# Low-rank attention of a two-layer kernel: score matmuls as 64-row pairs, four banks for key scores and three shared ones, 1024-column exponentials, softmax totals inverted as 128x8 through DMA

## The chip, the cores and the metric

The kernel runs on one core of a Trainium2 chip, as one program. The metric is the device time of one execution in microseconds; lower is better. TensorE is called PE below, VectorE DVE, ScalarE ACT, GpSimd POOL, and SyncE (which issues DMAs) SP.

## What is computed

Two layers over x of shape (8, 1024, 128): a window attention with 16 heads of 8 dimensions and a gated low-rank feed-forward part, then a low-rank attention and a feed-forward part whose input is quantised in blocks of 32. The change is in the second layer's attention. The reference has batches of (b, s) = (8, 1024) there and 8 heads:

```python
c_q = h_t @ W_DQ + b_DQ
c_kv = h_t @ W_DKV + b_DKV
q_c = (c_q @ W_UQ + b_UQ)...; k_c = (c_kv @ W_UK + b_UK)...; v_c = (c_kv @ W_UV + b_UV)...
q_r = (c_q @ W_QR + b_QR)...; k_r = (h_t @ W_KR + b_KR)   # the same for all heads
scores = jnp.einsum('bhsd,bhtd->bhst', concat(q_c, q_r), concat(k_c, k_r)) / sqrt(160)
attn = jax.nn.softmax(scores, axis=-1)
o = jnp.einsum('bhst,bhtd->bhsd', attn, v_c)
return o.reshape(b, s, 1024) @ W_O + b_O
```

The kernel folds the up-projections into the queries and into the output weights, so that a head's score is a product over 64 numbers (32 of c_kv and 32 of k_r) plus a constant for each query, and a head's result has 32 numbers before the output projection. Queries and keys stand as a high and a low part in a reduced-precision float, whose products are added.

## The kernel before

The program is written engine by engine, with semaphores between the queues; each queue runs in the order in which it is written. The gated part and the window attention take the first 580 us or so; the low-rank attention takes the rest and is the part that changes. In it the kernel goes through 64 heads u = 0..63 (8 batches of 8), each in 8 tiles of 128 keys, so that step g = 8u + t is tile t of head u. A plan (`low_rank_plan`) adds to the steps the small work of the other parts of the layer: "turn", "low", "const" and "value" prepare the next batch, "proj" is the output projection, "quant" and "product" the feed-forward part, "norm" and "quantise" their normalisations.

In step g each engine does the following:

- PE computes row scores (`pe_row_scores`, L1825) 14 steps ahead (`ROW_LEAD`), with the queries on the partitions: two matmuls of 512 columns for each tile of 128 queries. From them only the maximum over the keys is taken. It computes the key scores of step g (`pe_key_scores`, L1878 and L1882), with the keys on the partitions: for each half of the queries one matmul over 128 rows (high and low key parts against the high query part) and one over 65 rows (high key part against the low query part, and a row of ones against the shift). Every fourth step it weighs the values with four tiles of exponentials (`pe_weigh`, L1936), and at t = 3 of the next head it also sums the exponentials of a head over the keys ("total", L1929), which the plan places ahead of that weighing.
- DVE takes the maxima (`dve_row_max`, L1833, two per step), gathers them (`dve_row_top`, L1841), makes the low query part (L1754), inverts the totals (`dve_invert_totals`, L1946) and normalises (`dve_normalise`, L1953).
- ACT takes the exponentials (L1893, two per tile of 512 queries each) and copies the high query part out of PSUM (L1702).
- POOL adds seven of the head's eight tiles of exponentials in six additions (`pool_sum`, L1904 and L1907), and computes the shift (L1853, L1857).
- SP moves the shift into a row (`sync_move_shift`, L1864, 4 DMAs for each half of a head) and the normalised head into place (`sync_move_head`, L1964, 4 DMAs).

PSUM has 8 banks of 512 columns. Key scores go round banks 0 to 2, weighed values are in 3, row scores and totals go round 4 to 6, and bank 7 holds a query product or one of the small items. A matmul waits until the bank's last user has been read (`row_bank_free`, `low_bank_free`). Query products (L1641) are made 16 and 12 steps ahead, one half each.

## Time and profile before

| | |
|---|---|
| median of 3 runs | 1809.59 us (1809.46 to 1812.57) |
| profiled execution | span 1812.5 us; its own time is that of the slowest run shown, 1812.57 us |
| busy share of the span | PE 92%, PE weight loads 67%, DVE 77%, ACT 63%, POOL 65% |
| granted TensorE clock, mean | 0.967 of full speed |

A busy PE is not a PE at its peak: a 512-column matmul is shown as about 0.40 us while the next one starts 0.23 us later. So the cost of PE work is read below from the distance between two starts, and the same holds for DVE and ACT, whose instructions overlap a little as well.

### The profile page before, as it was taken

The page shows a single profiled execution, that of the slowest core. Times are in us where ns is not written, and L with a number is a line of the kernel's source. Part 1 is how long each engine was busy: PE and PEld are TensorE (multiplying, and loading weights), DVE is VectorE, ACT ScalarE, POOL GpSimd, SP SyncE. Part 2 cuts the span into 40 slices and gives each one's busy share as a digit, 9 for nine tenths or more (in the row PEclk, how much of TensorE's full clock was granted, in tenths as well). Part 3 has the DMA queues.
Part 4 walks back from the last instruction along what each step waited for, and adds up shares of the span by engine and source line. Part 5 has one row for each costly group of instructions (what it writes and reads, how often), then busy time and mean ns, then how long its engine had stood idle before and what let it go on. Part 6 is the DMA issues. An engine that isn't in the chain of part 4 may idle for free.

```text
span 1812.5 us, 39662 instructions
## 1 busy us (share of the span) xinstructions
PE 1670.4 (92%) x15057; PEld 1223.0 (67%) x15057; DVE 1393.8 (77%) x2976; ACT 1137.5 (63%) x2222; POOL 1177.3 (65%) x909
## 2 busy tenths in 40 slices
PE   4679999999877899999999999999999999999995
PEld 4557777777766567666766766766676677677674
DVE  5557777766597888878888888888887888888862
ACT  5447777777676466666666666666656666665662
POOL 4300111000066498898898988989889898898892
PEclk9889999999887899999999999999999999999997
DMA  4556666654000000000000000001001000100101
GB/s 123 136 140 156 162 156 159 164 136 116 29 1 1 1 10 8 10 8 10 7 13 16 10 8 19 11 7 22 7 10 19 8 10 7 22 7 10 19 10 30
DMA packets 198677, 81.47 MB, mean 45 GB/s; under 512 B 152553, under 2 KB 177493, under 8 KB 198357
## 3 DMA queue, kind: packets, MB, share of 16 engines
q1 hardware_dynamic: 198484, 78.93, 19.5%
q8 instruction: 119, 1.95, 0.5%
q14 instruction: 74, 0.60, 0.1%
HBM read 39.79 MB, written 29.88 MB: 38 GB/s over the span
## 4 chain that ended last, share of the span: by engine, by line
PE 54%; DVE 11%; POOL 2%; issue 1%; ACT 1%; DMA 0%; SPq 0%; POOLq 0%; ACTq 0%
PE pair L1825 12%; PE pair L1878 11%; PE pair L1882 11%; PE pair L1936 10%; DVE amax L1833 4%; PE pair L1929 4%; PE pair L1650 2%; DVE o_inv L1946 1%; PE pair L1641 1%; DVE stats L485 1%; POOL w_mix L1907 1%; PE pair L1664 1%; DVE q_low L1754 1%; DVE cq L1765 1%; DVE key_hl L1768 1%
## 5 line engine op out<-in xcount | busy, mean ns | idle before, releaser
L1893 ACT ACTIVATE prob<-pair 128x512 f32<-128x512 f32 x1024 | 604.4, 597 | 422.2 <-PE pair L1882 359.6
L1833 DVE TENSOR_REDUCE amax<-pair 128x1 f32<-128x512 f32 x1024 | 670.3, 682 | 133.9 <-PE pair L1825 131.8
L1825 PE MATMUL pair<-key_hl,q_hi 128*128 128x512 f32 x1024 | 437.8, 430 | 11.2 <-DVE amax L1833 7.1
L1878 PE MATMUL pair<-q_hi,key_hl 128*128 128x512 f32 x1024 | 405.2, 396 | 2.6 <-ACT prob L1893 2.6
L1882 PE MATMUL pair<-q_low,key_h 65*128 65x512 f32 x1024 | 406.0, 396 | 0.0
L1907 POOL TENSOR_TENSOR w_mix<-w_mix,prob 128x1024 f32<-128x1024 f32 x160 | 382.3, 2389 | 25.2 <-ACT prob L1893 8.5
L1907 POOL TENSOR_TENSOR Wm<-Wm,prob 128x1024 f32<-128x1024 f32 x155 | 369.6, 2384 | 20.8 <-ACT prob L1893 4.1
L520 POOL TENSOR_SCALAR veps<-mv 128x8 f32<-128x8 f32 x47 | 11.4, 243 | 452.6 <-DVE mv L493 451.2
L1825 PEld LDWEIGHTS pair<-key_hl,q_hi 128*128 128x128 f32 x1024 | 196.1, 192 | 115.9 <-issue 51.0
L1936 PE MATMUL pair<-prob,values 128*32 128x256 f32 x4096 | 247.2, 382 | 0.0
L1186 DVE TENSOR_REDUCE mx_neg<-pair 128x4 f32<-128x512 f32 x256 | 164.9, 687 | 94.8 <-PE pair L1090 94.1
L1878 PEld LDWEIGHTS pair<-q_hi,key_hl 128*128 128x128 f32 x1024 | 195.5, 191 | 44.3 <-ACT prob L1893 9.4
L1882 PEld LDWEIGHTS pair<-q_low,key_h 65*128 65x128 f32 x1024 | 192.5, 188 | 44.6
L1936 PEld LDWEIGHTS pair<-prob,values 128*32 128x32 f32 x4096 | 127.5, 110 | 100.9 <-issue 25.0
L1136 ACT ACTIVATE yT<-pair 128x512 f32<-128x512 f32 x256 | 138.6, 593 | 72.3 <-PE pair L1042 70.3
L1946 DVE RECIPROCAL o_inv<-pair 128x256 f32<-128x256 f32 x64 | 112.5, 1758 | 59.8 <-PE pair L1929 59.8
L542 ACT ACTIVATE y<-x,mean_neg,rstd 128x128 f32<-128x128 f32 x336 | 137.7, 485 | 19.0 <-POOL mean_neg L528 18.9
L1090 PE MATMUL pair<-keys,queries 64*128 64x128 f32 x1024 | 100.5, 317 | 0.0
L1042 PE MATMUL pair<-queries,keys 64*128 64x128 f32 x1024 | 97.0, 309 | 0.0
L1702 ACT ACTIVATE q_hi<-pair 128x512 fp32r<-128x512 f32 x128 | 75.7, 591 | 20.0 <-PE pair L1641 20.0
L1754 DVE TENSOR_TENSOR q_low<-pair,q_hi 64x512 fp32r<-64x512 f32 x128 | 86.3, 675 | 2.2 <-ACT q_hi L1702 2.2
L1090 PEld LDWEIGHTS pair<-keys,queries 64*128 64x128 f32 x1024 | 82.7, 199 | 3.7
(209 smaller groups left out, 2232.8 us busy)
## 6 DMA issues: line engine op xcount, KB each, us to landing
rows_mem<-once SPq DMA_DIRECT2D x128, 128.0 KB, 2.0
queries<-rows_mem SPq DMA_DIRECT2D x64, 256.0 KB, 4.5
keys<-rows_mem SPq DMA_DIRECT2D x16, 1024.0 KB, 7.1
rows_mem<-once SPq DMA_DIRECT2D x128, 64.0 KB, 1.9
q_low<-shift_cols SPq DMA_DIRECT2D x512, 0.5 KB, 2.0
yT<-o_norm SPq DMA_DIRECT2D x256, 32.0 KB, 1.9
x<-x_dram SPq DMA_DIRECT2D x8, 512.0 KB, 7.3
out_dram<-x SPq DMA_DIRECT2D x7, 512.0 KB, 3.4
```

Source lines behind the costliest of these rows:

```text
L542: ins = e.activation(y_of(stage, b)[:, t, :], x[:, b * NT + t, :], ACT.Identity, bias=mean_neg[:, k, t:t + 1], scale=rstd[:, k, t:t + 1])
L1090: ins = e.matmul(bank(S_BANKS[r])[:, q * P:(q + 1) * P], queries[rows, hb % QUERY_BUFS, q, m].rearrange("p s w -> p (s w)"), keys[rows, b ...
L1136: e.activation(pT[:, u % P_TURNED].rearrange("p q k -> p (q k)"), key_row_bank(*divmod(u, 2)), ACT.Exp).then_inc(*exps.up(u))
L1186: e.tensor_reduce(mx_neg[:, hb % 2, r, :, m], bank(S_BANKS[r]).rearrange("p (q k) -> p q k", q=QUADS), AX_X, ALU.max, negate=True).then_in ...
L1825: e.matmul(row_bank(("row", r, i)), q_hi[:, k, t * P:(t + 1) * P], key_hl[:, b % 2, i * HALF:(i + 1) * HALF], start=True, stop=True, skip_ ...
L1833: e.tensor_reduce(amax1[:, u % 2, t, i:i + 1], row_bank(("row", r, i)), AX_X, ALU.max).then_inc(*row_maxed.up((r, i)))
L1878: e.matmul(bank(j), key_hl[:, b % 2, ks], q_hi[:, k, sl], start=True, stop=False, skip_group_check=True)
L1882: e.matmul(bank(j), key_h1[:, b % 2, ks], q_low[:, k, sl], start=False, stop=True, skip_group_check=True).then_inc(*key_scored.up((g, half)))
L1893: e.activation(prob1[:, g % P_BUFS, half * HALF:(half + 1) * HALF], bank(K_BANKS[(2 * g + half) % 3]), ACT.Exp, scale=SCALE1).then_inc(*ke ...
L1907: e.tensor_tensor(into, into, p, ALU.add).then_inc(*summed_keys.up(g))
L1936: ins = e.matmul(bank(PVB)[q * DC:(q + 1) * DC, 0:QUARTER], values[:, b % 2, t, :], prob1[:, g % P_BUFS, q * QUARTER:(q + 1) * QUARTER], s ...
L1946: e.reciprocal(o_inv[:, u % 2, :], row_bank(("total", u, 0))[:, 0:QUARTER]).then_inc(*o_inverse.up(u))
```

## The change

It touches the low-rank stage alone.

- **Layout.** The two halves of the 1024 queries stand above each other: `q_hi` and `q_low` are 128x512, with the first 512 queries on partitions 0 to 63 and the others on 64 to 127. `key_high` and `key_low` hold the 64 key rows twice. The shift has a tile of its own, `q_shift`, in which row 0 and row 64 hold it, and is added by a matmul against ones.
- **Scores.** All score matmuls take 64 rows and come in pairs, one on partitions 0 to 63 and one on 64 to 127, into two banks. Row scores are one pair per step where they were two full matmuls (they use the high parts alone); key scores are four pairs (high by high, low key, low query, shift) where they were two full matmuls and two of 65 rows. One query product of two accumulated matmuls serves a whole head, 17 steps ahead.
- **Banks.** Key scores of step g use two banks (0 and 1, or 2 and 3), weighed values are in 4. Banks 5 to 7 are shared in turn by row scores, totals, queries and all small items. Small items now stand only at t = 3: one ahead of the total, one behind the weighing.
- **Exponentials.** One of 1024 columns per tile, which waits for both sides.
- **Additions.** POOL adds six of the eight tiles in five additions; PE sums three parts for the total where it summed two.
- **Totals.** For all heads but the last two ACT copies totals and weighed values to SBUF. SP moves the totals into 128x8 (4 DMAs), DVE inverts that, SP stores it to DRAM (1), waits for it, and loads it back spread over 4x32 partitions (4); then DVE multiplies. Line numbers of the changed kernel in what follows: L1858 row scores, L1920 key scores, L1867 maxima, L1783 `q_low`, L2010 inversion, L2028 normalisation.

The core of the diff:

```diff
-PIPELINE = 16
+PIPELINE = 17
+PVB, SHARED_BANKS = 4, (5, 6, 7)
+SUMMED = 6
...
+    def use(key):
+        places[key] = SHARED_BANKS[len(uses) % 3], uses[-3] if len(uses) >= 3 else None
+        uses.append(key)
+        return places[key]
...
-        if item is None and waiting and (g % 2 == 0 or g >= NT * U):
+        if item is None and waiting and (g >= NT * U or g % NT == 3 and waiting[0][0] != "low"):
...
+        def pe_row_scores(e, r):
+            u, t, half = row_tiles(r)
+            b, k = u // NH, u % Q_BUFS
+            e.wait_ge(*q_hi_done.at((u, 0)))
+            if r % (NT * NH) == 0:
+                e.wait_ge(*key_copied.at((b, 1)))
+            for side in range(2):
+                shared_bank_free(e, ("row", r, side))
+            for side in range(2):
+                rows = slice(side * KR, (side + 1) * KR)
+                e.matmul(shared_bank(("row", r, side)), q_hi[rows, k, t * P:(t + 1) * P],
+                         key_high[rows, b % 2, half * HALF:(half + 1) * HALF], start=True, stop=True,
+                         skip_group_check=True).then_inc(*row_scored.up((r, side)))
...
+        def pe_key_scores(e, g):
...
+            if g >= 2:
+                e.wait_ge(*key_exp.at(g - 2))
+            for part in range(4):
+                if t == 0 and part == 2:
+                    e.wait_ge(*q_lo_done.at((u, 0)))
+                if t == 0 and part == 3:
+                    e.wait_ge(*shift_ready(u))
+                for side in range(2):
+                    rows = slice(side * KR, (side + 1) * KR)
+                    weights = ones_shift[rows, :] if part == 3 else (key_low if part == 1 else key_high)[rows, b % 2, ks]
+                    moving = (q_hi, q_hi, q_low, q_shift)[part][rows, k, :]
+                    ins = e.matmul(banks[side], weights, moving, start=part == 0, stop=part == 3, skip_group_check=True)
...
+        def act_copy_total(e, u):
+            e.wait_ge(*totalled.at(u))
...
+        def sync_move_total(e, u):
+            e.wait_ge(*total_copied.at(u))
+            for q in range(4):
+                e.dma_start(total_cols[q * DC:(q + 1) * DC, u % 2, :],
+                            total_rows[q * DC:q * DC + 1, u % 2, :].rearrange("o (p t) -> o p t", t=NT)).then_inc(
+                    total_moved[u % 2], 16)
+        def dve_invert_spread(e, u):
+            e.wait_ge(total_moved[u % 2], 64 * (u // 2 + 1))
+            e.reciprocal(inverse_cols[:, u % 2, :], total_cols[:, u % 2, :]).then_inc(*spread_inverse.up(u))
+        def sync_move_inverse(e, u):
+            e.wait_ge(*spread_inverse.at(u))
+            e.dma_start(inverse_mem[u % 2].rearrange("(p t) -> p t", t=NT), inverse_cols[:, u % 2, :]).then_inc(
+                inverse_stored[u % 2], 16)
+            e.wait_ge(inverse_stored[u % 2], 16 * (u // 2 + 1))
+            for q in range(4):
+                e.dma_start(o_inv[q * DC:(q + 1) * DC, u % 2, :],
+                            inverse_mem[u % 2, q * QUARTER:(q + 1) * QUARTER].unsqueeze(0).broadcast_to([DC, QUARTER])
+                            ).then_inc(inverse_moved[u % 2], 16)
+        def dve_normalise_spread(e, u):
+            e.wait_ge(inverse_moved[u % 2], 64 * (u // 2 + 1))
+            e.wait_ge(*o_copied.at(u))
...
+                if t == 3 and 0 <= u and spread_out(u):
+                    dve_invert_spread(e, u)
+                if t == 7 and 0 <= u and spread_out(u):
+                    dve_normalise_spread(e, u)
...
             for u in range(B * NH + 2):
                 if u < B * NH:
-                    for i in range(2):
-                        sync_move_shift(e, u, i)
+                    sync_move_shift(e, u)
                 if u >= 2:
+                    if spread_out(u - 2):
+                        sync_move_total(e, u - 2)
+                        sync_move_inverse(e, u - 2)
                     sync_move_head(e, u - 2)
```

What this does to the order, at three places. First SP, in the middle of the stage; `yT<-o_norm` moves a normalised head, `q_low<-shift_cols` moves a shift. Before, two heads:

```order
L1964 DMA yT<-o_norm 32x256 x4
L1864 DMA q_low<-shift_cols 1x128x1 x8
L1964 DMA yT<-o_norm 32x256 x4
L1864 DMA q_low<-shift_cols 1x128x1 x8
L1964 DMA yT<-o_norm 32x256 x4
```

And now, two heads from the same part of the program:

```order
L2046 DMA yT<-o_norm 32x256 x4
L1898 DMA q_shift<-shift_cols 1x128x1 x8
L2004 DMA total_cols<-total_rows 32x1x8 x4
L2015 DMA inverse_mem<-inverse_cols 128x8
L2019 DMA o_inv<-inverse_mem 32x256 x4
L2046 DMA yT<-o_norm 32x256 x4
L1898 DMA q_shift<-shift_cols 1x128x1 x8
L2004 DMA total_cols<-total_rows 32x1x8 x4
```

Per head there are 21 DMAs where there were 12, and between the moves of the shift and those of the head stand the three steps of the inversion. In `sync` the shift that follows head u's normalisation is that of head u + 3, and the totals behind it are those of head u + 1.

Second DVE, one head before:

```order
L1833 TENSOR_REDUCE amax<-pair 128x1 x4
L1946 RECIPROCAL o_inv<-pair 128x256
L1953 TENSOR_TENSOR o_norm<-pair,o_inv 128x256
L1833 TENSOR_REDUCE amax<-pair 128x1 x4
L1841 TENSOR_REDUCE shift<-amax 128x4
L1754 TENSOR_TENSOR q_low<-pair,q_hi 64x512
L1833 TENSOR_REDUCE amax<-pair 128x1 x8
L1841 TENSOR_REDUCE shift<-amax 128x4
L1754 TENSOR_TENSOR q_low<-pair,q_hi 64x512
```

And now:

```order
L2028 TENSOR_TENSOR o_norm<-o_raw,o_inv 128x256
L1867 TENSOR_REDUCE amax<-pair 128x1 x8
L2010 RECIPROCAL inverse_cols<-total_cols 128x8
L1867 TENSOR_REDUCE amax<-pair 128x1 x6
L1783 TENSOR_TENSOR q_low<-pair,q_hi 128x512
L1867 TENSOR_REDUCE amax<-pair 128x1 x2
L1874 TENSOR_REDUCE shift<-amax 128x8
L2028 TENSOR_TENSOR o_norm<-o_raw,o_inv 128x256
```

The inversion stands between the fourth and the fifth pair of maxima after a normalisation, in front of the maxima of that step, and the multiplication four steps later. One `q_low` per head stands between the seventh and the eighth pair.

Third PE, at a query product. Before, with the waits (`row_half_maxima` is the end of a maximum on DVE, `query_low` that of `q_low`):

```order
L1878 MATMUL pair<-q_hi,key_hl 128x512 [waits key_exponentials]
L1882 MATMUL pair<-q_low,key_h 128x512 [waits shift_row_1_last_half]
L1641 MATMUL pair<-cq,w_query 128x512 [waits keys_ready]
L1825 MATMUL pair<-key_hl,q_hi 128x512 [waits row_half_maxima]
L1878 MATMUL pair<-q_hi,key_hl 128x512 [waits key_exponentials]
L1882 MATMUL pair<-q_low,key_h 128x512
L1825 MATMUL pair<-key_hl,q_hi 128x512 [waits row_half_maxima]
L1878 MATMUL pair<-q_hi,key_hl 128x512 [waits key_exponentials]
```

And now, from the row scores behind the product and the weighing on:

```order
L1858 MATMUL pair<-key_high,q_hi 128x512 [waits row_half_maxima]
L1858 MATMUL pair<-key_high,q_hi 128x512
L1920 MATMUL pair<-q_hi,key_high 128x512 [waits key_exponentials]
L1920 MATMUL pair<-q_hi,key_high 128x512
L1920 MATMUL pair<-q_hi,key_low 128x512 x2
L1920 MATMUL pair<-q_low,key_high 128x512 x2
L1920 MATMUL pair<-q_shift,ones_shift 128x512 x2
L1858 MATMUL pair<-key_high,q_hi 128x512 [waits row_half_maxima,query_low]
L1858 MATMUL pair<-key_high,q_hi 128x512
```

Before, a query product had bank 7 to itself and no row score waited for it; now the second pair of row scores behind it takes its bank.

## Rows read from the trace of the kernel before

**Rows 1.** Busy time by engine (PE, PEld, DVE, ACT, POOL), clock; attention stage.

```profile
700.00:1750.00 1050.00, 1032.91 (x7965) 722.80 (x7958) 876.47 (x1554) 663.06 (x1199) 939.76 (x650) 1.00 0.08 12
```

**Rows 2.** Groups of instructions by line, 700 to 1750 us.

```profile
L1833 DVE TENSOR_REDUCE amax<-pair 128x1 f32<-128x512 f32 x914 | 599.1, 682 | 118.8 <-PE pair L1825 116.9
L1893 ACT ACTIVATE prob<-pair 128x512 f32<-128x512 f32 x914 | 541.7, 597 | 377.0 <-PE pair L1882 319.1 <-POOL Wm L1904 6.1
...
L1946 DVE RECIPROCAL o_inv<-pair 128x256 f32<-128x256 f32 x57 | 100.2, 1758 | 34.0 <-PE pair L1929 34.0
L1754 DVE TENSOR_TENSOR q_low<-pair,q_hi 64x512 fp32r<-64x512 f32 x114 | 76.9, 675 | 0.0
...
L485 DVE BATCH_NORM_STATS2 stats<-x 128x6 f32<-128x128 f32 x104 | 22.0, 274 | 0.0
...
L1768 DVE SCALAR_TENSOR_TENSOR key_hl<-pair,Wt,key_hl 64x512 fp32r<-64x512 f32 x12 | 8.9, 744 | 0.4
```

**Rows 3.** The write of o_norm: all 64, then two in the timeline.

```profile
L1953 DVE TENSOR_TENSOR o_norm<-pair,o_inv x64: 405/425/427, 637.3 to 1785.5; 128x256 f32<-128x256 f32 x64
...
709.17 0.42 DVE L1953 TENSOR_TENSOR o_norm<-pair,o_inv 128x256 f32<-128x256 f32 x1
...
725.82 0.42 DVE L1953 TENSOR_TENSOR o_norm<-pair,o_inv 128x256 f32<-128x256 f32 x1
```

**Rows 4.** Timeline of PE round a total and a weighing.

```profile
1202.60 0.39 PE L1878 MATMUL pair<-q_hi,key_hl 128*128 128x512 f32 x1
1202.83 0.39 PE L1882 MATMUL pair<-q_low,key_h 65*128 65x512 f32 x1
1203.14 0.64 PE L1929 MATMUL pair<-prob,ones_col 128*32 128x256 f32 x8
...
1204.03 1.91 PE L1936 MATMUL pair<-prob,values 128*32 128x256 f32 x32
1205.87 0.50 PE L1825 MATMUL pair<-key_hl,q_hi 128*128 128x512 f32 x1
1206.21 0.39 PE L1878 MATMUL pair<-q_hi,key_hl 128*128 128x512 f32 x1
```

**Rows 5.** Timeline of PE in the window stage, 64-row matmuls.

```profile
301.87 0.39 PE L1085 MATMUL pair<-mask_bf,both_rows 64*128 64x512 bf16 x2 [0.17 <-DVE mx_neg L1186]
301.90 0.74 PE L1090 MATMUL pair<-keys,queries 64*128 64x128 f32 x8
302.49 0.39 PE L1035 MATMUL pair<-both_rows,mask_bf 64*128 64x512 bf16 x2
```

**Rows 6.** Timelines of PE and DVE: row scores and their maxima.

```profile
1196.41 0.50 PE L1825 MATMUL pair<-key_hl,q_hi 128*128 128x512 f32 x1
...
1196.94 1.39 DVE L1833 TENSOR_REDUCE amax<-pair 128x1 f32<-128x512 f32 x2 [1.02 <-PE pair L1825]
...
1201.53 2.46 DVE L1833 TENSOR_REDUCE amax<-pair 128x1 f32<-128x512 f32 x4
...
1202.26 0.50 PE L1825 MATMUL pair<-key_hl,q_hi 128*128 128x512 f32 x1 [0.46 <-DVE amax L1833]
```

**Rows 7.** Timelines of DVE and SP, then DMA issues with us to landing.

```profile
1152.77 0.42 DVE L1953 TENSOR_TENSOR o_norm<-pair,o_inv 128x256 f32<-128x256 f32 x1
...
1153.22 2.47 SPq L1964 DMA_DIRECT2D yT<-o_norm  x4
...
1158.52 2.46 SPq L1864 DMA_DIRECT2D q_low<-shift_cols  x4
...
q_low<-shift_cols SPq DMA_DIRECT2D x512, 0.5 KB, 2.0
yT<-o_norm SPq DMA_DIRECT2D x256, 32.0 KB, 1.9
```

**Rows 8.** PE after a long wait, and the clock of that stretch (columns of rows 1).

```profile
364.06 0.61 PE L1085 MATMUL pair<-mask_bf,both_rows 64*128 64x512 bf16 x2 [2.73 <-DMA keys<-rows_mem]
...
364.00:370.70 6.70, 6.64 (x68) 5.27 (x70) 1.59 (x3) 2.76 (x7) 0.48 (x3) 0.50 0.50 123
```

More of the change, by code:

```diff
@@ L265, in low_rank_plan @@
     while g < NT * U + 26 or running or waiting:
-        early, late = [], []
+        early, late, after = [], [], []
         b, r = divmod(g, NT * NH)
@@ L1636, in pe_low_part @@
                 return
-            low_bank_free(e, before)
+            if item not in places_m or before:
+                low_bank_free(e, before)
             if kind == "query":
@@ new lines, in sync_move_shift @@
+        def sync_move_shift(e, u):
+            e.wait_ge(*shift_steps.at((u, 2)))
+            queries_free(e, u)
+            if u == 0:
+                e.wait_ge(*set_low.at("shift rows"))
+            for t in range(NT):
+                side, n = divmod(t, NT // 2)
+                e.dma_start(q_shift[side * KR:side * KR + 1, u % Q_BUFS, n * P:(n + 1) * P].bitcast(F32).rearrange(
+                    "o (p t) -> o p t", t=1), shift_cols[:, t:t + 1].bitcast(F32)).then_inc(
+                    shift_moved[u % Q_BUFS], 16)
@@ L1822, in pe_row_scores @@
+        def pe_key_scores(e, g):
+            u, t = divmod(g, NT)
+            b, k = u // NH, u % Q_BUFS
+            ks = slice(t * P, (t + 1) * P)
+            banks = [bank(g % 2 * 2 + side) for side in range(2)]
             if u % NH == t == 0:
                 e.wait_ge(*keys_done.at((b, 1)))
-            row_bank_free(e, ("row", r, i))
-            e.matmul(row_bank(("row", r, i)), q_hi[:, k, t * P:(t + 1) * P], key_hl[:, b % 2, i * HALF:(i + 1) * HALF],
-                     start=True, stop=True, skip_group_check=True).then_inc(*row_scored.up((r, i)))
@@ L1896, in pool_sum @@
+        def act_exponentials(e, g):
+            if g >= P_BUFS:
+                before = g - P_BUFS
+                e.wait_ge(*pv_done.at(before // 4))
+                if before % NT < SUMMED:
+                    e.wait_ge(*summed_keys.at(max(before % NT, 1) + before // NT * NT))
+            for side in range(2):
+                e.wait_ge(*key_scored.at((g, side)))
+            e.activation(prob1[:, g % P_BUFS, :], pair[g % 2][:, :], ACT.Exp, scale=SCALE1).then_inc(*key_exp.up(g))
         def pool_sum(e, g):
@@ L1993, in pe_low_rank @@
             e.wait_ge(*x_dve.at(("c", B - 2)))
-            for g, early, late in plan_m:
+            e.wait_ge(*keys_done.at((0, 1)))
+            for g, early, late, after in plan_m:
                 if g == CONST_AT:
@@ L2013, in pe_low_rank @@
                     pe_weigh(e, g // 4 - 1)
+                for (item, j, before), part in after:
+                    pe_low_part(e, item, j, before, part)
         def act_low_rank(e):
-            for g, early, late in plan_m:
+            for g, early, late, after in plan_m:
                 if g == LAST_C["copy"]:
@@ L2056, in dve_low_rank @@
         def dve_low_rank(e):
-            for g, early, late in plan_m:
+            for g, early, late, after in plan_m:
                 if g == CONST_AT + 1:
```

313 lines of the change are left out of this document (155 added, 158 removed).

## The prediction

> **What bounds the kernel now.** I read the table by stages first. In the steady part of the low-rank stage, 1050 of the 1812 us, PE is busy for 1033 us at the full clock; DVE is busy for 876, ACT 663, POOL 940 [rows 1] (the row gives the length, then busy us and instructions of PE, PEld, DVE, ACT and POOL, then the clock). Then I looked at what one head costs. The 64 normalisations start from 637.3 to 1785.5 us, 18.2 us apart on average, and two heads without small items are 16.65 us apart [rows 3]. Does PE's own work explain these 16.65 us? A 512-column matmul follows the last one after 0.23 us, a total costs 0.89 us (1203.14 to 1204.03), and a weighing 2.03: from the start at 1202.83 to the one at 1206.21 are 3.38 us, less 0.89 and two ordinary slots [rows 4]. A head has 16 row-score, 32 key-score and 2 query matmuls: 50 x 0.233 = 11.65, two weighings 4.06, a total 0.89, together 16.6. So a plain head waits for nothing. PE sets the pace, and the 1.6 us on top are small items with a few waits.
>
> **What the change takes from PE and adds.** The window stage has 64-row pairs already. Two 512-column matmuls of 64 rows lie within 0.39 us, the time of one, and the eight of 128 columns behind them take 0.74 us in four pairs, their weights loaded while the columns of the pair before run [rows 5]. I take 0.233 us for a pair of 512 columns, as for one full matmul. Bounds: not below this, since one matmul has that pace, and twice as much if pairs should not run side by side. Per head: row scores go from 16 slots to 8 (-1.87 us), key scores stay at 32 slots, the query at 2; the third part of the total costs half of 0.89 (+0.44). PE's part falls by 1.4 us to about 15.2 per plain head. Five additions in place of six and the cheap reciprocal relieve POOL and DVE (L1946 is 1.76 us, [rows 2]), which did not set the pace. The exponential of 1024 columns costs between one and two of 0.60 us [rows 2]; I take 1.0. With two pairs of banks, key scores of step g+2 can start 2.2 us after those of g (three slots, 0.44, 1.0, 0.05), while PE needs 2 x 1.17 = 2.33 for two steps. That is hidden.
>
> **What it adds in waits: DVE and three banks.** A maximum starts 0.03 us after the row score's end, so about 0.44 after its start (0.53 for the long one behind a weighing), four maxima take 2.46 us, so 0.60 from one to the next, and PE goes on 0.06 us after the end of the maximum that it waited for [rows 6]. A step of PE is now 5 x 0.233 = 1.17 us and its two maxima take 1.20, where before a step had 1.40. DVE has no room left between two weighings, and row scores, totals, queries and items share three banks. The eighth pair of row scores takes the query's bank, so it waits for `q_low`, which is queued behind the seventh pair's maxima: 0.44 + 2 x 0.60 + 0.68 + 0.06 = 2.38 us after the seventh pair, where PE would be there after 1.17. That stalls PE, and with it the next key scores, for 1.2 us per head. By the same steps the second pair behind a normalisation comes 0.55 late (gathering and normalisation stand ahead of the maxima), and the total, the query and the last pair before it 0.25, 0.25 and 0.15. These 2.4 us turn 15.3 into 17.7, more than the 16.65 of now.
>
> **What it adds in waits: one queue for all DMAs.** This is the larger part. Four DMAs keep SP for 2.47 us, 0.62 each, and land 1.9 to 2.0 us after their issue; the first starts 0.45 us after the start of the normalisation that it waits for [rows 7]. Let N be the start of one head's normalisation. Behind it SP issues 4 moves of the head, 8 of the next shift (ready by then, since its maxima stand ahead of N), and only then the 4 of the next head's totals. The last of the 16 is issued at N + 0.45 + 15 x 0.62 = N + 9.75 and has landed at N + 11.75, so DVE inverts at N + 11.8 at the earliest. By its own work it would be there at N + 8.3 in a plain head (my count: 4.9 us to the end of the weighing, two steps, their maxima and the queue before it). DVE waits 3.5 us. What is queued behind the wait is the fifth pair of maxima, for which PE's sixth pair waits, and all of PE with it.
>
> From the inversion I to the next normalisation there is no slack either. The store and its return and the four loads take 0.15 + 2.1 + 1.9 + 2.0 = 6.2 us, but the engines need more: the fifth pair's first maximum ends at I + 0.78 and its second at 1.38, query from 1.44 to 1.9, weighing to 3.95, key scores to 4.9, seventh pair's maxima and `q_low` to 7.2, eighth pair at 7.25, its maxima from 7.7 to 9.0, gathering, next normalisation at I + 9.1. A head therefore takes 11.8 + 9.1 = 20.9 us. Small items stand in the first part and mostly fit under SP's 11.8; the projection's two items of 1.8 us just fill it.
>
> **The sum.** Normalisations 0 to 61 go through DRAM: 61 distances x (20.9 - 18.2) = 165 us. Items that stand in the DVE part or don't fit: 14 heads with a "low" item, whose bank waits for three operations of 0.74 us [rows 2], 1.5 us each beyond SP's time; 14 heads with eight statistics and their aggregation, 1.3 us each (eight x 0.19 of the 0.27 us shown [rows 2], half of it ahead of `q_low`, and 0.5): 39 us. PE now stands still for about 3.7 us in each head. Behind a wait of 2.73 us the clock fell to half, the lower level of 1.2 GHz, for 6.7 us [rows 8]. Its price is between nothing and the 3.4 us that PE works between I and the seventh pair, x 61; since the fall comes late there and SP's part has slack at its end, I take 0.4 per head, 24 us. Total: 1812.5 + 165 + 39 + 24 = 2040 us; the profiled execution is 3 us above the median, which I leave.
>
> The Trainium skill's page "TensorE: Matmul & The Clock Gate" (section "Why this matters for your kernels") advises against idle gaps mid-kernel because the clock falls behind them; by it the 24 us would be nearer the upper bound than nothing.
>
> **The rivals.**
> - *Only the banks count* (0.12): DMAs are issued faster than I think, or the inversion is in time. Then heads take 17.7, with their items 20.3 on average (the 1.6 of now, 0.3 for switches between shapes and 1.0 for the items that share banks): 1812.5 + 61 x 2.1 = 1940. For it: the DMA's own time is short. Against it: 0.62 us of SP per DMA in every row. The Trainium skill's page "DMA: Bandwidth & Descriptors", section "Issuing engines are not separate DMA queues", calls the time to initiate a DMA usually small relative to the DMA itself. By that rule SP's chain would be three landings of 2 us and this rival would hold; the trace has 0.62 against 2.0, times sixteen.
> - *The clock falls in every head on the path* (0.12): 61 x 1.7 more instead of 24: about 2120.
> - *Pairs do not overlap* (0.03): 40 slots more per head, 9.3 us, part of it under the waits: about 2400. Rows 5 speak against it.
> - *PE stays the bound* (0.05): DVE's waits are hidden and a head costs PE's 15.3 us where it cost 16.6: 64 x 1.3 gives 1730. It needs both the wait for `q_low` (1.2 us, almost the whole gain) and the wait for the totals gone. The point that decides: 11.8 + 9.1 would have to be below 18.2, so SP below 0.45 us per DMA.
> - *Gains and waits cancel* (0.01): within 0.2%, about what a measurement of this kernel can tell from no change.
>
> **How the numbers follow.** The forecast, 0.67, has its own range of 1990 to 2090: the SP part by 0.60 to 0.65 us per DMA, the clock from nothing to 1.2 us per head. With the banks-only case and the clock case on either side the range for eight in ten is 1930 to 2130. Faster 0.05, same 0.01, slower 0.94: every other case is slower.
>
> **What would show it.** Normalisations (L2028) about 21 us apart. Reciprocals (L2010) late, their idle time put down to the DMA `total_cols`, some 3 us per head. SP with almost no wait for the shift, where issues of L2046, L1898 and L2004 stand in one row of 16 over 10 us. PE idle in front of L1858, once per head for 3 to 4 us with maxima as releaser (the step of the inversion), and once for 1.2 us with `q_low` as releaser. L1858 and L1920 in pairs, 0.23 us from pair to pair. The granted clock below 1.0 in this stage if the clock's term is there. I am wrong if heads are under 18.2 us apart, if DMAs behind one another cost SP much less than 0.6 us, or if the 16 issues don't stand between a normalisation and the next inversion.

## The result, and the profile after

The changed kernel takes 2137.6 us, the median of 4 runs (2129.2 to 2146.1), beside 1809.5 us for the kernel before (1805.7 to 1812.6): 1.181 times, with a 95% interval of 1.177 to 1.185. It is slower by 328 us. The forecast was 2040 us with a range of 1930 to 2130, so the direction was right and the time lies just above the range. The profiled execution has a span of 2127.2 us.

The windows first, with the columns of [rows 1] (the last two are for later), then the groups by line over 700 to 1750 us, and the two kinds of normalisation (count: shortest, median and longest in ns, first and last start).

```profile
700.00:1750.00 1050.00, 880.68 (x8126) 559.30 (x8128) 591.91 (x1158) 487.70 (x629) 617.94 (x378) 0.94 0.09 15
...
1521.80:1525.40 3.60, 1.01 (x4) 0.52 (x4) 1.88 (x4) 1.02 (x1) 3.46 (x2) 0.98 0.04 4
1525.40:1529.00 3.60, 3.60 (x33) 1.35 (x32) 0.77 (x2) 0.60 (x1) 0.22 (x1) 0.54 0.23 41
```

```profile
L1867 DVE TENSOR_REDUCE amax<-pair 128x1 f32<-128x512 f32 x718 | 460.5, 683 | 324.1 <-PE pair L1858 318.3
L1932 ACT ACTIVATE prob<-pair 128x1024 f32<-128x1024 f32 x358 | 366.4, 1024 | 340.7 <-PE pair L1920 333.0
...
L1783 DVE TENSOR_TENSOR q_low<-pair,q_hi 128x512 fp32r<-128x512 f32 x45 | 30.5, 679 | 0.0
...
L2010 DVE RECIPROCAL inverse_cols<-total_cols 128x8 f32<-128x8 f32 x45 | 9.0, 199 | 56.1 <-DMA total_cols<-total_rows 56.0
```

```profile
L2028 DVE TENSOR_TENSOR o_norm<-o_raw,o_inv x62: 389/424/427, 664.2 to 2085.3; 128x256 f32<-128x256 f32 x62
L2035 DVE TENSOR_TENSOR o_norm<-pair,o_inv x2: 415/420/424, 2088.4 to 2098.7; 128x256 f32<-128x256 f32 x2
```

In [rows 1] every engine but PE had idle time and PE had almost none: 1033 of 1050 us. Now PE is busy for 881, and no engine is full. 718 maxima fit in the stretch where 914 did [rows 2]. A maximum costs what it did, 683 ns; the exponential of 1024 columns costs 1.02 us; the reciprocal fell from 1.76 us to 0.20. The work is cheaper and the time is longer, so it went into waiting. The 61 distances between the normalisations of L2028 are 23.3 us on average (2085.3 less 664.2); over the same heads they were 18.4 before, and 61 times the difference is 302 us of the 328.

What PE waits for in that stretch (line waited for: us in total, times, longest):

```profile
PE pair L1858 <- DVE amax L1867: 74.1, 69, 3.8
PE pair L1858 <- DVE q_low L1783: 55.6, 45, 1.8
PE pair L1858 <- DVE key_low L1798: 30.1, 11, 2.7
PE pair L1858 <- ACT total_rows L1991: 7.0, 10, 0.7
```

And the timeline of one head on SP's queue, DVE and PE, from its normalisation at 1510.31 to the next at 1534.39:

```profile
1510.76 2.44 SPq L2046 DMA_DIRECT2D yT<-o_norm  x4
1513.30 6.24 SPq L1898 DMA_DIRECT2D q_shift<-shift_cols  x8
1519.58 2.50 SPq L2004 DMA_DIRECT2D total_cols<-total_rows  x4
1523.70 0.34 SPq L2015 DMA_DIRECT2D inverse_mem<-inverse_cols  x1
1525.13 2.52 SPq L2019 DMA_DIRECT2D o_inv<-inverse_mem  x4
...
1510.31 0.42 DVE L2028 TENSOR_TENSOR o_norm<-o_raw,o_inv 128x256 f32<-128x256 f32 x1
...
1523.47 0.20 DVE L2010 RECIPROCAL inverse_cols<-total_cols 128x8 f32<-128x8 f32 x1 [2.64 <-DMA total_cols<-total_rows]
...
1534.39 0.42 DVE L2028 TENSOR_TENSOR o_norm<-o_raw,o_inv 128x256 f32<-128x256 f32 x1
...
1524.37 0.50 PE L1858 MATMUL pair<-key_high,q_hi 64*128 64x512 f32 x2 [2.58 <-DVE amax L1867]
...
1525.71 3.38 PE L1974 MATMUL pair<-prob,values 128*32 128x256 f32 x32
```

SP issues sixteen DMAs in one piece, from 1510.76 to 1522.08, and DVE stands before the inversion until the last of them has landed. PE's row scores stand behind that in turn: at 1524.37 they start after 2.58 us with the maxima as releaser. Then the clock is at its lower level: the last two windows have 0.98 ahead of 1525.4, where PE is busy for 1.01 of 3.60 us, and 0.54 behind it. The weighing there takes 3.38 us, where one at the full clock takes 1.94 (at 1514.11 in the same head). In what follows N is a normalisation, I the next inversion and N' the next normalisation; these distances are worked out from the start times of L2028 and L2010 in the traces, as means over the 61 normalisations whose next head goes through DRAM. A head's number h is u mod 8, counted at N.

### The profile page after: what moved, and what is told of

It reads as the page before. It is cut to its first block, busy times and chain, and to the rows that moved or that the text cites. A ratio compares the mean times of both kernels' runs of the same rounds, so it can differ in the third digit from the quotient of the medians.

```text
span 2127.2 us, 45092 instructions
## 1 busy us (share of the span) xinstructions
PE 1761.2 (83%) x17673; PEld 1208.2 (57%) x17673; DVE 1255.8 (59%) x2865; ACT 1089.7 (51%) x1770; POOL 1011.5 (48%) x719
## 4 chain that ended last, share of the span: by engine, by line
PE 39%; SPq 22%; DVE 16%; issue 8%; DMA 7%; ACT 5%; POOL 4%; POOLq 0%; ACTq 0%; DVEq 0%
SPq L1898 10%; PE pair L1974 9%; PE pair L1920 8%; DVE amax L1867 7%; PE pair L1858 6%; SPq L2046 4%; DMA total_cols<-total_rows 3%; SPq L2004 3%; DMA keys<-rows_mem 3%; DVE q_low L1783 2%; PE pair L1967 2%; ACT y L556 2%; PE pair L1665 2%; SPq L966 1%; PE pair L1676 1%
## 5 line engine op out<-in xcount | busy, mean ns | idle before, releaser
L1867 DVE TENSOR_REDUCE amax<-pair 128x1 f32<-128x512 f32 x1024 | 656.8, 683 | 467.9 <-PE pair L1858 459.6
L1932 ACT ACTIVATE prob<-pair 128x1024 f32<-128x1024 f32 x512 | 523.5, 1024 | 474.4 <-PE pair L1920 463.4
L1858 PE MATMUL pair<-key_high,q_hi 64*128 64x512 f32 x1024 | 257.5, 490 | 243.6 <-DVE amax L1867 116.1
L1858 PEld LDWEIGHTS pair<-key_high,q_hi 64*128 64x128 f32 x1024 | 111.5, 197 | 398.7 <-DVE amax L1867 180.1
L1920 PE MATMUL pair<-q_hi,key_high 64*128 64x512 f32 x1024 | 231.0, 436 | 0.9 <-ACT prob L1932 0.9
L1920 PE MATMUL pair<-q_shift,ones_shift 64*128 64x512 f32 x1024 | 216.4, 407 | 0.7 <-DMA q_shift<-shift_cols 0.7
L1920 PE MATMUL pair<-q_low,key_high 64*128 64x512 f32 x1024 | 216.0, 406 | 0.0
L1920 PE MATMUL pair<-q_hi,key_low 64*128 64x512 f32 x1024 | 215.2, 405 | 0.0
L556 ACT ACTIVATE y<-x,mean_neg,rstd 128x128 f32<-128x128 f32 x336 | 137.5, 483 | 20.3 <-POOL mean_neg L542 20.3
L1920 PEld LDWEIGHTS pair<-q_hi,key_high 64*128 64x128 f32 x1024 | 105.6, 194 | 61.3 <-issue 50.2
L1920 PEld LDWEIGHTS pair<-q_shift,ones_shift 64*128 64x128 f32 x1024 | 107.1, 193 | 18.9 <-DMA q_shift<-shift_cols 1.1
L1920 PEld LDWEIGHTS pair<-q_low,key_high 64*128 64x128 f32 x1024 | 107.1, 194 | 18.6
L1920 PEld LDWEIGHTS pair<-q_hi,key_low 64*128 64x128 f32 x1024 | 108.0, 196 | 11.9
```

What stands on the lines that cost most here:

```text
L556: ins = e.activation(y_of(stage, b)[:, t, :], x[:, b * NT + t, :], ACT.Identity, bias=mean_neg[:, k, t:t + 1], scale=rstd[:, k, t:t + 1])
L1858: e.matmul(shared_bank(("row", r, side)), q_hi[rows, k, t * P:(t + 1) * P], key_high[rows, b % 2, half * HALF:(half + 1) * HALF], start=Tr ...
L1867: e.tensor_reduce(amax1[:, u % 2, NT // 2 * side + t, half:half + 1], shared_bank(("row", r, side)), AX_X, ALU.max).then_inc(*row_maxed.up ...
L1920: ins = e.matmul(banks[side], weights, moving, start=part == 0, stop=part == 3, skip_group_check=True)
L1932: e.activation(prob1[:, g % P_BUFS, :], pair[g % 2][:, :], ACT.Exp, scale=SCALE1).then_inc(*key_exp.up(g))
```

## The experiments

Each kernel is the changed kernel with the edit shown. The first four test SP's queue from four sides.

**no_spread** undoes the inversion by DMA alone.

```diff
-            return u < B * NH - 2
+            return False
```

> The changed kernel without the spreading of the totals: DVE takes the reciprocal of 128x256 out of PSUM and normalises as before, so SP issues 12 DMAs per head and nothing else of the change is undone (64-row pairs, four key banks, three shared banks, 128x1024 exponentials, five additions stay). Theory (SP's single queue sets the period of 23.3 us from normalisation to normalisation): the period falls to what the banks allow, about 18 to 19 us, and the time is 1940 us (1870 to 1980). Rival (the coupling through the three shared banks, not SP, cost most of the 314 us): the time stays above 2050 us.

Measured: 1965.3 us, 1.085 times before (1.083 to 1.087). Of the loss of 328 us, 172 go with the spreading and 154 stay. The time is within the theory's range, 25 us above its number, and both halves are larger than forecast (100 and 130).

**one_dma** keeps the bytes and makes one DMA of four, twice.

```diff
-            for q in range(4):
-                e.dma_start(total_cols[q * DC:(q + 1) * DC, u % 2, :],
-                            total_rows[q * DC:q * DC + 1, u % 2, :].rearrange("o (p t) -> o p t", t=NT)).then_inc(
-                    total_moved[u % 2], 16)
+            e.dma_start(total_cols[:, u % 2, :], total_rows[0:P:DC, u % 2, :].rearrange("q (p t) -> q p t", t=NT)
+                        ).then_inc(total_moved[u % 2], 16)
...
-            for q in range(4):
-                e.dma_start(o_inv[q * DC:(q + 1) * DC, u % 2, :],
-                            inverse_mem[u % 2, q * QUARTER:(q + 1) * QUARTER].unsqueeze(0).broadcast_to([DC, QUARTER])
-                            ).then_inc(inverse_moved[u % 2], 16)
+            e.dma_start(o_inv[:, u % 2, :], inverse_mem[u % 2].rearrange("(q o x) -> q o x", q=4, o=1).broadcast_to(
+                [4, DC, QUARTER])).then_inc(inverse_moved[u % 2], 16)
```

> The changed kernel with the four DMAs of the totals written as one and the four loads of the inverse written as one: SP issues 15 DMAs per head instead of 21, same bytes, same buffers. Theory (SP's issues ahead of the inversion, 16 of 0.62 to 0.70 us, set the time from a normalisation to the next inversion): three issues fewer there, 12.84 us falls by about 1.9 to 11.0 us, the three loads fewer are hidden behind the four steps from inversion to normalisation: 61 x 1.9 = 115 us less, 2020 us (1980 to 2060). Rival (the latency of the round trip through DMA and memory sets it, not the issues): the time stays at 2130 us or above, since one DMA with as many packets lands no earlier.

Measured: 2036.7 us, 101 us less. One head on SP:

```profile
1338.61 2.47 SPq L2042 DMA_DIRECT2D yT<-o_norm  x4
1341.18 5.64 SPq L1898 DMA_DIRECT2D q_shift<-shift_cols  x8
1346.87 0.61 SPq L2003 DMA_DIRECT2D total_cols<-total_rows  x1
1348.99 0.32 SPq L2013 DMA_DIRECT2D inverse_mem<-inverse_cols  x1
```

One DMA to 128 partitions costs SP 0.61 us, as much as one to 32 partitions does, and from its issue at 1346.87 to the store behind the inversion pass 2.1 us. In these rows the count of issues has a price, not the bytes. N to I fell only in heads 3 to 7, by 1.6 us (table below); in heads 0 to 2 it hardly moved. I to N' fell by 0.5 us, and no weighing is at half clock any more (see the clock below).

**act_totals** takes the four issues off SP.

```diff
                     act_copy_weighed(e, u)
+                    sync_move_total(e, u)
...
                     if spread_out(u - 2):
-                        sync_move_total(e, u - 2)
```

> The changed kernel with the four DMAs of the totals issued by ACT right behind its two copies, so that they no longer stand behind the heads' four and the shift's eight on SP. Theory (the order on SP's queue makes the inversion late): the time from normalisation to inversion falls from 12.8 us to about 9 us, the period from 23.3 to about 19.5 us, and the time is 1900 us (1850 to 1960); ACT holds its exponentials for some 2.4 us per head, which its half-idle time mostly covers. Rival (the round trip itself is too long wherever it is issued): the time stays above 2060 us.

Measured: 2063.4 us, 74 us less, by its size on the rival's side. Its mechanism is not the rival's, though. The inversion no longer waits (6.5 us in 1050 where it was 56.0), and yet N to I only falls to 10.5 us in heads 3 to 7, not to 9: DVE has not come by. And ACT now issues:

```profile
1321.09 0.38 ACT L1999 ACTIVATE o_raw<-pair 128x256 f32<-128x256 f32 x1 [1.34 <-PE pair L1975]
1321.09 2.44 ACTq L2005 DMA_DIRECT2D total_cols<-total_rows  x4
1323.65 1.95 ACT L1933 ACTIVATE prob<-pair 128x1024 f32<-128x1024 f32 x2 [2.18 <-PE pair L1921]
```

The last row puts the 2.18 us down to PE, whose scores end at 1323.23 by its timeline; the exponential starts 0.4 us later, when the four issues are through. Here that is small. In other heads the scores are complete early in the four issues, the exponential starts up to 2.8 us late, and PE's next key scores, which need its banks, then wait for ACT. PE's waits over 700 to 1750 us, and one of them:

```profile
PE pair L1921 <- ACT prob L1933: 28.2, 20, 2.0
...
1304.32 0.50 PE L1921 MATMUL pair<-q_hi,key_high 64*128 64x512 f32 x2 [1.69 <-ACT prob L1933]
```

No such wait stands in the changed kernel or in totals_first in this stretch. With the pairs at half clock, 0.6 us per head where totals_first pays 0.4, this is about what act_totals stays behind totals_first, 31 us.

**totals_first** leaves all 21 DMAs on SP and changes their order.

```diff
             for u in range(B * NH + 2):
+                if u >= 2 and spread_out(u - 2):
+                    sync_move_total(e, u - 2)
                 if u < B * NH:
                     sync_move_shift(e, u)
                 if u >= 2:
                     if spread_out(u - 2):
-                        sync_move_total(e, u - 2)
                         sync_move_inverse(e, u - 2)
```

> The changed kernel with SP's order altered: the four DMAs of the totals stand ahead of the eight of the next head's shift, the inverse's store and loads behind them; all 21 DMAs stay. Theory (not their number but the eight ahead of the totals make the inversion late): the time from normalisation to inversion falls from 12.8 to about 9.5 us (the totals are copied some 4.6 us after the normalisation, 2.5 us of issues, 2 us of landing), the store goes behind the shift, still in time for the next normalisation; the shift lands later but ahead of its head's key scores: 1990 us (1950 to 2050). Rival (SP's 21 issues by their sum are the bound, in whatever order): 2110 us or above.

Measured: 2032.5 us, 105 us less, with the same DMAs. So the sum of SP's issues is not the bound; that eight of them stand ahead of the totals is. The inversion waits for 3.9 us in 1050 here. It is in the theory's range but 42 us above its number, and N to I again stops at 10.4 us in heads 3 to 7 where 9.5 was forecast for all. The shift didn't always land ahead of its key scores, as the theory had it: PE waits for it twelve times in the stretch, 11.4 us in all.

**q_low_early** tests the coupling through the banks.

```diff
-            elif kind == "query" and part == 3:
+            elif kind == "query" and part == 2:
                 e.wait_ge(*q_hi_done.at((a, i)))
```

> The changed kernel with DVE's subtraction that makes q_low, and that frees the query's bank, one step earlier (in the step in which ACT copies q_hi). SP's chain is untouched. Theory (SP's chain sets the time from normalisation to inversion, PE's steps set that from inversion to normalisation): PE's wait of 1.24 us per head for that subtraction lies ahead of the normalisation, so up to 61 x 1.2 = 75 us can go, and the wait for maxima takes back a part: 2090 us (2060 to 2120). Rival (the bank coupling sets the whole period): the same 75 us and more goes, 2060 us or below, and the time from normalisation to inversion falls too. Rival (the loads of the inverse set when the next normalisation comes): no change, 2130 to 2145 us.

Measured: 2061.1 us, 76 us less. I to N' fell from 10.4 to 9.5 us, and N to I stayed (12.4 and 13.5 us). So SP's chain and this wait are in series, as the prediction added them. **banks_qlow** is the same edit on top of no_spread.

> The changed kernel without spreading (no_spread, 1965 us) and with q_low one step earlier (q_low_early). Theory (without SP's chain PE's steps and the coupling of the three banks set the whole period, and in no_spread PE still waits 1.23 us per head for q_low): the 1.2 us per head go whole, 61 x 1.2 = 73 us less than 1965: 1890 us (1875 to 1910). Rival (the wait moves on to the maxima behind it): 1950 us or above.

Measured: 1889.0 us, 76 less than no_spread: much the same with and without SP's chain. That the two numbers are equal is luck, since the four times of the changed kernel lie between 2129 and 2146 us and the profiled executions differ by 60 and 68 us. What is left against the kernel before is 83 us (1889.0 beside 1806.1 on that chip), and it isn't in the plain heads. Mean distance in us from the normalisation of head h to the next, for h = 0 to 7, worked out from the start times of 55 heads, without the first and last few:

```
before      20.8 19.7 19.2 17.4 17.0 17.8 18.0 17.6
banks_qlow  21.7 17.4 23.0 23.8 17.2 19.6 17.4 17.5
```

Heads 2 and 3, in which most of the "low" items, the constants and the values stand, carry 10.2 us more per sequence. **banks_early** moves DVE's part of a low item one step forward, `part == 3` to `part == 2` in the same function.

> As banks_qlow, and DVE's three instructions that split the keys (cq, key_low twice) one step earlier too, so that the shared bank of a low item comes free sooner. Theory (the items, not the plain heads, carry what the shared banks cost beside q_low: in no_spread heads 2 and 3 of each sequence take 23.7 and 24.5 us where the plain ones take 18.4 to 18.9, and PE waits 2.77 us for key_low twelve times in 1000 us): up to 2 us for each of the 14 low items go, 28 us less than banks_qlow: 1862 us (1850 to 1885). Rival (those heads are long by the work of the items on PE and ACT, and the wait for key_low only moves): within 8 us of banks_qlow.

Measured: 1890.7 us, nothing gained, as the rival said. The wait changed its name: PE waited 33.2 us for `key_low` and 14.4 for maxima in banks_qlow, here 46.2 for maxima. **keys_short** shortens the work instead of moving it.

```diff
+                if a >= 2:
+                    sl = slice(i * HALF, i * HALF + 8)
                 for rows in (slice(0, KR), slice(KR, P)):
-                    ins = e.scalar_tensor_tensor(out=key_low[rows, k, sl], in0=bank(j)[0:KR, :], scalar=b_low[0:KR],
+                    ins = e.scalar_tensor_tensor(out=key_low[rows, k, sl], in0=bank(j)[0:KR, 0:sl.stop - sl.start], scalar=b_low[0:KR],
```

> As banks_qlow (1889 us), with DVE's two subtractions that make key_low cut to 8 of 512 columns from the third sequence on (the rest of key_low keeps old values, so the output is not the reference's): a low item's bank comes free some 1.3 us sooner. Theory (a low item costs PE its wait of 2.77 us and, behind the wait, pairs at half clock, 0.43 us in place of 0.23, for 3 to 5 us): the wait halves and the clock often holds, 12 items x (1.35 + up to 1.7) = 16 to 37 us less: 1860 us (1850 to 1875). Rival (only DVE's time counts or the wait only moves to the maxima, as in banks_early): 1880 us or above.

Measured: 1868.1 us, 21 less. The longest wait for `key_low` falls from 2.8 to 1.7 us, 12.7 us in all. The rest goes with the clock: by their distances, pairs at half clock cost banks_qlow 23 us and this kernel 12. So at least 21 of the 83 us are this hold of a bank; the other 62 were not traced to a cause. In banks_qlow, PE behind such a wait (two lines of its timeline), and the two windows round it:

```profile
1158.92 0.50 PE L1858 MATMUL pair<-key_high,q_hi 64*128 64x512 f32 x2 [2.77 <-DVE key_low L1798]
...
1160.29 0.71 PE L1858 MATMUL pair<-key_high,q_hi 64*128 64x512 f32 x2
1160.74 0.68 PE L1920 MATMUL pair<-q_hi,key_high 64*128 64x512 f32 x2
```

```profile
1157.00:1160.30 3.30, 1.38 (x12) 0.90 (x12) 2.66 (x5) 1.71 (x4) 3.16 (x2) 1.00 0.04 10
1160.30:1163.70 3.40, 3.40 (x16) 2.45 (x14) 2.32 (x4) 2.69 (x4) 2.70 (x2) 0.52 0.00 0
```

Behind the wait the next pairs are 0.43 us apart in place of 0.23, at a granted clock of 0.52, the lower level. Over 700 to 1750 us the clock is 0.98 in banks_qlow and 1.00 in keys_short.

**pv_total** (on banks_qlow) writes the totals into the free half of the weighed values' bank, behind the weighing, and takes them out of the rotation of the shared banks.

```diff
-            use(("total", g // NT - 1, 0))
...
-                        done = e.matmul(shared_bank(("total", u, 0))[q * DC:(q + 1) * DC, 0:QUARTER], ones_col[:, :],
+                        ins = e.matmul(bank(PVB)[q * DC:(q + 1) * DC, QUARTER:2 * QUARTER], ones_col[:, :],
```

> As banks_qlow (no spreading, q_low early, 1889 us), with the totals in the second half of the bank of the weighed values, behind those matmuls, so that they no longer take a turn in the rotation of the three shared banks. Theory (beside q_low and the items the rotation costs little: PE waits only 14 us in 1000 for maxima there): 5 to 20 us less, 1877 us (1865 to 1887). Rival (the reciprocal of 1.76 us holding a shared bank is a main cost of the three banks): 1850 us or below. Rival (behind the weighed values the reciprocal makes the normalisation, and so the next weighing, late): above 1895 us.

Measured: 1908.3 us, 19 more; the theory is wrong and the second rival right. The reciprocal now waits for the end of the weighing, 134.6 us in 1050 where it waited for its totals for 50.3. Since the edit also makes the reciprocal late, it doesn't show what the totals' turn in the rotation costs by itself; it shows that taking them out in this way costs more than it gives.

**few_dmas** and **spread_best** ask whether spreading can be free. few_dmas has the edits of one_dma and q_low_early, and POOL issues the shift.

```diff
                     pool_shift(e, r // NT - 1)
+                    sync_move_shift(e, r // NT - 1)
...
-                if u < B * NH:
-                    sync_move_shift(e, u)
```

> The changed kernel with the totals in one DMA and the inverse's load in one (one_dma), q_low one step earlier (q_low_early), and the eight DMAs of the shift issued by POOL behind its subtraction, so that SP issues 7 per head: 4 for the head, 1 total, 1 store, 1 load. Theory (the spreading costs what it costs by SP's queue alone): the inversion comes when PE's steps bring it (8.3 to 9 us behind the normalisation), the spreading is hidden and the time is that of banks_qlow, 1890 us (1875 to 1930), if POOL's issues cost it no more than its idle time. Rival (the round trip through DMA and memory is long by itself, or POOL's issues hold up its additions): above 1960 us.

Measured: 1981.0 us, the rival's side. POOL is busy for 912.5 of 1050 us, and its issues are a large group:

```profile
L1899 POOL DMA_DIRECT2D q_shift<-shift_cols x400 | 214.4, 543 | 24.4 <-POOL shift_cols L1889 14.8 <-issue 9.6
```

What ACT's exponentials waited for in the same stretch, by the releaser that came last:

```profile
ACT prob L1933 <- POOL Wm L1946: 14.3, 10, 2.5
ACT prob L1933 <- POOL w_mix L1943: 14.3, 5, 3.1
```

Eight issues take 4.3 us of POOL per head. These two rows are not the price, though: banks_qlow, 92 us faster, has 46.3 us of the same waits in the same stretch, and in few_dmas no exponential of the stretch starts more than 0.45 us after the scores that it needs as well. What the next kernel, with the shift back on SP, doesn't have is PE's wait for POOL's sums ahead of a total, 12 us over the whole stage, and it has 20 us less of PE's waits for maxima; it is 39 us faster. How POOL's issues make the maxima late was not followed. spread_best keeps the shift on SP and combines one_dma, totals_first and q_low_early.

> The changed kernel, spreading kept, with three edits: totals in one DMA and the inverse's load in one (one_dma), that one DMA of the totals ahead of the next head's shift on SP (totals_first), q_low one step earlier (q_low_early). SP has 15 issues per head, one of them ahead of the inversion. Theory (SP's issues ahead of the inversion are all that the spreading costs, and POOL's own load was what few_dmas paid above 1889): the store goes out behind the shift, 11 to 12 us behind the normalisation, its load lands before 16, and PE's steps set the pace: the time is near that of banks_qlow (1889 us), 1905 us (1885 to 1930). Rival (the spreading costs by its round trip as well): 1950 us or above.

Measured: 1941.7 us, between the two. SP is out of it: DVE waits for `total_cols` once in the whole trace. ACT is in it. Its rows behind a "turn" item:

```profile
1295.96 0.60 ACT L1734 ACTIVATE yT<-pair 128x512 f32<-128x512 f32 x1 [3.39 <-PE pair L1696]
1296.46 0.38 ACT L1991 ACTIVATE total_rows<-pair 128x256 f32<-128x256 f32 x1
1296.72 0.39 ACT L1998 ACTIVATE o_raw<-pair 128x256 f32<-128x256 f32 x1
1297.20 1.03 ACT L1932 ACTIVATE prob<-pair 128x1024 f32<-128x1024 f32 x1
```

The totals are ready in their bank 2.8 us before ACT copies them, because the copy of an item whose matmul comes behind the weighing stands ahead. **act_order** turns that round on top of spread_best.

```diff
-                for (item, j, before), part in early:
-                    act_low_part(e, item, j, before, part)
                 u, t = divmod(g - 12, NT)
                 if t == 0 and 0 <= u and spread_out(u):
                     act_copy_total(e, u)
-                    act_copy_weighed(e, u)
+                for (item, j, before), part in early:
+                    act_low_part(e, item, j, before, part)
                 if 0 <= g < total:
                     act_exponentials(e, g)
+                if t == 0 and 0 <= u and spread_out(u):
+                    act_copy_weighed(e, u)
```

> As spread_best (1942 us, SP no longer waited for), with ACT's order altered in the step behind the totals: the copy of the totals ahead of an item's copy, the copy of the weighed values behind the exponential instead of ahead of it. Theory (the 52 us that spread_best keeps above banks_qlow's 1889 come from ACT's in-order queue: the totals' copy stands behind an item's copy while PE waits for the bank, 12 waits of 0.7 us in 1000 us, and the exponential stands behind the copy that waits for the weighed values): 1942 falls to 1925 us (1910 to 1935). Rival (the rest lies with DVE, whose step that normalises is one that the bank coupling cannot hide): 1937 us or above.

Measured: 1916.8 us, 25 less. The same item and totals:

```profile
1282.64 0.39 ACT L1991 ACTIVATE total_rows<-pair 128x256 f32<-128x256 f32 x1 [2.85 <-PE pair L1967]
1282.93 0.59 ACT L1734 ACTIVATE yT<-pair 128x512 f32<-128x512 f32 x1
1284.94 0.60 ACT L1734 ACTIVATE yT<-pair 128x512 f32<-128x512 f32 x1 [1.42 <-PE pair L1696]
```

The distances that go with these times, in us (heads 3 to 7 and 0 to 2 apart for the first part):

```
kernel        N to I, 3-7  N to I, 0-2  I to N'  sum of means
changed          12.4         13.5       10.4     23.3
one_dma          10.8         13.3        9.9     21.7
act_totals       10.5         13.2       10.6     22.1
totals_first     10.4         13.1       10.2     21.7
q_low_early      12.4         13.5        9.5     22.3
spread_best      10.3         13.1        8.9     20.3
act_order        10.2         12.5        8.8     19.9
```

## Where the prediction was right, and where it failed

**The direction, and both mechanisms.** SP's single queue and the coupling through the shared banks were named as the two costs, they add up in series, and undoing either gives back what it costs. The time is 97 us above the forecast of 2040. What follows goes through the terms of the sum.

**PE's own part.** The exponential of 1024 columns was taken as 1.0 us and is 1.02; pairs follow one another after 0.23 us. In banks_qlow, where neither the chain of DMAs nor the wait for `q_low` stands, plain heads need 17.2 to 17.5 us, about as before; by the sum it would have been 17.7 - 1.2 = 16.5. What makes the rest was not tried.

**The coupling, 2.4 us per head.** The wait for `q_low` was forecast at 1.2 us per head and is 55.6/45 = 1.24. The banks-only case was put at 1940; no_spread shows 1965. Most of these 25 us are a slip of addition: 17.7 + 1.6 + 0.3 + 1.0 is 20.6 us per head and not 20.3, which gives 1959, and no_spread shows 20.7. That rival had no term for the clock either, and pairs at half clock cost no_spread 22 us, so its other terms were some 16 us too high together.

**SP's part, 11.8 us from N to I.** Measured in heads 3 to 7: 12.4. The last issue starts at N + 10.6 in place of 9.75. The step that is off is "four DMAs keep SP for 2.47 us, 0.62 each", carried over to all sixteen: the eight of the shift take 5.58 us on average, 0.70 each. This is 0.6 us in five heads of eight, 23 us in all.

**"By its own work it would be there at N + 8.3", so "DVE waits 3.5 us".** This step failed too. With SP out of the way DVE is there at 10.3 to 10.5 in the mean of heads 3 to 7; head 6 alone, which has no small item, comes near with 8.9 to 9.2. SP's wait was therefore 56.1/45 = 1.2 us per head, not 3.5. The 105 us that totals_first gives back is close to the 100 forecast for SP, and this is in part luck: 61 times 1.2 is 76 us, and some 23 more are the weighings behind the wait, which return to the full clock.

**"Small items stand in the first part and mostly fit under SP's 11.8."** This is the step that failed by most. Heads 0 to 2 take 13.5 us from N to I, and still 13.1 in spread_best, where SP is not waited for: 1.7 us beyond 11.8 in three of eight heads, some 42 us in all, where the sum had 21 for the low items. In heads 1 and 2 (14.0 and 13.6) the path is that of PE and DVE and not SP's: fourteen times, all but one in these heads, PE waits about 2.7 us for `key_low`, 38 us in all. Behind the wait shown here the pairs are at half clock for about 3.4 us, and the inversion comes without a wait.

```profile
1289.24 0.51 PE L1858 MATMUL pair<-key_high,q_hi 64*128 64x512 f32 x2 [2.74 <-DVE key_low L1798]
...
1290.25 0.65 PE L1920 MATMUL pair<-q_low,key_high 64*128 64x512 f32 x2
1290.68 0.65 PE L1920 MATMUL pair<-q_shift,ones_shift 64*128 64x512 f32 x2
...
1290.98 0.19 DVE L2010 RECIPROCAL inverse_cols<-total_cols 128x8 f32<-128x8 f32 x1
```

Behind I, 9.1 us were forecast and heads 3 and 4 show 9.3 and 9.7, but the mean is 10.4, some 82 us in all, where the sum had 18 for the statistics beside the clock. The two parts together are 2.4 us longer than 20.9, where the terms for items and clock made 1.0. The difference, 83 us over the 61 heads, is most of the missing 97: about 25 of it the clock, 23 SP's issues and the rest the items, of which the part behind I was not taken apart further. The last 14 us lie outside these 61 distances and between the profiled execution and the median.

**The clock, 0.4 us per head.** Too low by half. Pairs at half clock cost 0.4 us per head, and the weighing behind I about as much again: 16 of 128 weighings take over 2.5 us by the distance of their first and last start, where one at the full clock takes 1.52. That makes some 49 us in place of 24. Such weighings are frequent only in the two of these runs in which the sixteen issues stand whole (16 in changed, 19 in q_low_early, at most one in the others). The Trainium skill's page "TensorE: Matmul & The Clock Gate", section "Why this matters for your kernels", advises against such gaps; the trace agrees, and the price was between my bounds.

**What the sum had no term for: ACT.** The change gives ACT two copies per head. They are short, and I costed them at nothing without naming their cover. They stand in front of an exponential and behind item copies, and act_order gives back 25 us by order alone. 28 us remain between act_order and banks_qlow; what they are was not tried.

The Trainium skill's page "DMA: Bandwidth & Descriptors", section "Issuing engines are not separate DMA queues", calls the time to initiate a DMA usually small beside the DMA itself. That did not decide here: the trace has 0.61 us of issue against a landing of 2, and sixteen in a row.

No version beats the kernel before. The best that does the whole computation is banks_qlow, 1889 us; its 83 us lie in heads 2 and 3.

## What to carry to other kernels

In these runs a DMA of 0.5 KB keeps its queue for as long as one of 32 KB, mostly 0.5 to 0.6 us (0.34 for the store of the inverse to DRAM). What counts is how many issues stand between an event and the one that waits for it: reorder or merge there first (105 and 101 us here), and don't move issues to an engine whose own queue is on the path. When a transfer replaces an instruction, list every engine that gets a new in-order step from it and what is queued behind each one; short copies cost by where they stand. And when banks are shared, a forecast from plain steps is a floor: count the steps with small items one by one, with the clock behind each long wait.

## What the runs showed that I had not expected

The same eight DMAs of 0.5 KB cost SP 5.0 us in some heads and up to 6.4 in others; the four of 32 KB ahead of them mostly cost about 2.45. On ACT four cost 2.44, on POOL eight cost 4.3. And clock and wait make each other worse: in keys_short, 1.1 us off a wait brought the granted clock from 0.98 to 1.00 and 8 us more than the waits alone.
